# Dense products of an attention and FFN layer: one plain fp32 matmul per product in place of three matmuls of rounded high and low parts

## The reference

```
xn = layernorm(x)                                   # no gain, no bias
s  = attention(xn)                                  # 16 heads of 16, RoPE, causal softmax, q k v and output products 256x256
h  = fwht(xn * SU_ug) / 64                          # Walsh-Hadamard transform over 256
h  = silu(h @ W_gate.T * a) * (h @ W_up.T * b)      # 256 -> 1024
h  = fwht(h * SU_dp) / 64                           # over 1024
g  = silu(h @ W_down.T * c)                         # 1024 -> 256
out = x + s * g
```

## Time and profile before

| what | value |
|---|---|
| time, median of 3 runs | 804.27 us (802.99 to 805.4) |
| span of the profiled execution, first to last instruction | 804.6 us |
| busy in the span: PE, DVE, ACT, POOL | 787.2, 566.7, 497.8, 411.1 us |
| weight loads on PE | 482.7 us |
| mean granted TensorE clock | 0.993 |

### The profile page before, as it was taken

The page is one execution under the profiler, slowest core; times in us unless marked ns, Lnnn a source line. Parts: engine busy times, 40 slices in busy tenths (PEclk is TensorE's granted clock), DMA queues, the critical chain, the costliest instruction groups (busy, mean ns, idle before and its releaser), DMA issues. The chain is left out here.

```text
span 804.6 us, 14554 instructions
## 1 busy us (share of the span) xinstructions
PE 787.2 (98%) x5232; PEld 482.7 (60%) x5232; DVE 566.7 (70%) x1021; ACT 497.8 (62%) x686; POOL 411.1 (51%) x472
## 2 busy tenths in 40 slices
PE   8999999999999999999999999999999999999987
PEld 4678788888766555555555555555555555555545
DVE  5875545456686777777777777777777777777736
ACT  4576355463544777667777665677766677666472
POOL 3878678574742463321765434267453236746233
PEclk9999999999999999999999999999999999999997
DMA  9262444354541222333333453334344333445121
GB/s 319 84 199 96 158 156 158 106 131 145 182 113 39 65 77 60 91 107 107 103 107 110 122 171 93 95 108 132 115 114 142 98 105 95 133 130 170 67 87 70
DMA packets 61248, 95.71 MB, mean 119 GB/s; under 512 B 10553, under 2 KB 27641, under 8 KB 61177
## 3 DMA queue, kind: packets, MB, share of 16 engines
q1 hardware_dynamic: 59176, 92.42, 38.0%
q10 hardware_dynamic: 2000, 2.36, 0.9%
HBM read 57.54 MB, written 36.95 MB: 117 GB/s over the span
## 5 line engine op out<-in xcount | busy, mean ns | idle before, releaser
L1564 ACT ACTIVATE probs<-ps 128x1024 f32<-128x1024 f32 (+1 forms) x320 | 292.0, 938 | 93.7 <-PE ps L1391 92.0
L1686 DVE TENSOR_REDUCE mx<-ps 128x4 f32<-128x1024 f32 (+1 forms) x192 | 216.1, 1134 | 58.9 <-PE ps L1368 37.2
L1249 POOL TENSOR_SCALAR_AFFINE_SELECT probs<-probs 128x256 f32<-128x256 f32 (+1 forms) x192 | 92.6, 485 | 255.1 <-ACT probs L1564 254.5
L1681 DVE CUSTOM_DVE_ANT_0 ps<-ps,tri 128x512 f32<-128x512 f32 (+1 forms) x256 | 153.8, 652 | 48.4 <-PE ps L1368 48.3
L1413 PE MATMUL ps<-probs,v_ones 128*32 128x512 f32 (+3 forms) x1584 | 157.0, 486 | 0.1
L1391 PE MATMUL ps<-q_s,k_s 64*128 64x512 f32 (+3 forms) x768 | 143.7, 399 | 3.8 <-ACT probs L1564 1.4
L1368 PE MATMUL ps<-k_s,q_s 48*128 48x512 f32 (+3 forms) x768 | 134.7, 381 | 4.1 <-DVE mx L1686 0.8
L1391 PEld LDWEIGHTS ps<-q_s,k_s 64*128 64x128 f32 x768 | 67.0, 184 | 103.9 <-issue 53.6
L1368 PEld LDWEIGHTS ps<-k_s,q_s 48*128 48x128 f32 x768 | 69.5, 185 | 63.6 <-ACT probs L1564 38.2
L343 PE MATMUL ps<-xh,wug_hi 128*128 128x512 f32 x256 | 105.6, 413 | 1.0 <-DVE rot L898 1.0
L398 POOL TENSOR_TENSOR a_sb<-a_sb,u_sb 128x512 f32<-128x512 f32 x64 | 82.4, 1295 | 41.7 <-ACT u_sb L371 20.9
(11 more groups left out here) (151 smaller groups left out, 1061.5 us busy)
## 6 DMA issues: line engine op xcount, KB each, us to landing
scr_qk<-kinds SPq DMA_DIRECT2D x64, 256.0 KB, 2.4
q_s<-scr_qk SPq DMA_DIRECT2D x64, 128.0 KB, 2.8
k_s<-scr_qk SPq DMA_DIRECT2D x64, 128.0 KB, 3.0
scr_heads<-o_raw SPq DMA_DIRECT2D x30, 256.0 KB, 2.1
scr_v<-v_st SPq DMA_DIRECT2D x16, 256.0 KB, 2.9
q_s<-scr_qk SPq DMA_DIRECT2D x64, 64.0 KB, 3.0
k_s<-scr_qk SPq DMA_DIRECT2D x64, 64.0 KB, 3.1
v_raw<-scr_v SPq DMA_DIRECT2D x16, 256.0 KB, 2.8
```

Source lines behind the costliest of these rows:

```text
L1249: pool.affine_select(out=part, in_=part, compare_op=ALU.is_ge, fill=0.0, base=0, pattern=pattern, channel_multiplier=-1).then_inc(cut, 1)
L1564: act.activation(probs[:, n % 2, p, :, 0:w], ps[:, bank:bank + 2, 0:w], ACT.Exp, scale=SCALE).then_inc(exp_ok, 1)
L1681: last = dve.tensor_tensor_reduce(part_of, part_of, sh.tri[:, CH - w:CH], 1.0, LOWEST, ALU.add, ALU.max, mx[:, v % 2, kind, h, i % TPC:i % ...
L1686: last = dve.tensor_reduce(out[:, :, pairs[0]:pairs[0] + n], ps[:, banks[0]:banks[0] + 2, 0:n * w].rearrange('p e (x k) -> p e x k', x=n), ...
```

## The change

Every operand is kept once, in plain fp32: `wug`, `wd`, `wqkv`, `wo`, `wo_end`, `xt`, `hid`. Each product is one plain fp32 matmul. All roundings and subtractions that made the parts go, with their semaphores. `hidden` now writes to `hid` and takes over the wait for the downs of the FFN chunk before. `take_xh` becomes `take_x`, a copy in plain fp32 by ACT. The weights that were scratch views over other tiles (`late`, `res`) become tiles of their own or views of `wug`; the reload of x goes to `x_res`, after a wait for the results of the chunk before. The rounds, the jobs in them and the PSUM banks stay.

```diff
-        self.hid_hi = nc.alloc_sbuf_tensor_at('hid_hi', [P, IB, CH], F32R, offset=HID_AT)
-        self.hid_lo = nc.alloc_sbuf_tensor_at('hid_lo', [P, IB, CH], F32R, offset=HID_AT + 4 * IB * CH)
+        self.hid = sb('hid', [P, IB, CH])
...
-        self.wug_hi = sb('wug_hi', [P, DC, 2 * INTER], F32R)
-        self.wug_lo = sb('wug_lo', [P, DC, 2 * INTER], F32R)
-
-        self.late = nc.alloc_sbuf_tensor_at('late', [P, 5 * DC, CH], F32, offset=WUG_AT)
-        self.wd_hi = sb('wd_hi', [P, IB, D], F32R)
-        self.wd_lo = sb('wd_lo', [P, IB, D], F32R)
-        self.xh = sb('xh1', [P, DC, CH], F32R)
-        self.xl = sb('xl1', [P, DC, CH], F32R)
+        self.wug = sb('wug', [P, DC, 2 * INTER])
+        self.wd = sb('wd', [P, IB, D])
+        self.xt = sb('xt1', [P, DC, CH])
...
 def ffn_features(pe, ps, sh, bank, ib, first_col, done):
     cols = slice(first_col + ib * P, first_col + (ib + 1) * P)
-    terms = [(w, a, d) for d in range(DC)
-             for w, a in ((sh.wug_hi, sh.xh), (sh.wug_hi, sh.xl), (sh.wug_lo, sh.xh))]
-    for m, (w, a, d) in enumerate(terms):
-        last = pe.matmul(ps[:, bank, :], w[:, d, cols], a[:, d, :], start=m == 0, stop=m == len(terms) - 1)
+    for d in range(DC):
+        last = pe.matmul(ps[:, bank, :], sh.wug[:, d, cols], sh.xt[:, d, :], start=d == 0, stop=d == DC - 1)
     last.then_inc(done, 1)
 
 
 def ffn_down(pe, ps, sh, bank, n, o, q):
     per = IB // QUARTERS
-    pe.wait_ge(sh.hl_ok, nth_hid(n, per * (q + 1)))
+    pe.wait_ge(sh.hid_ok, nth_hid(n, per * (q + 1)))
     cols = slice(o * P, (o + 1) * P)
     for ib in range(per * q, per * (q + 1)):
-        for k, (w, h) in enumerate(((sh.wd_hi, sh.hid_hi), (sh.wd_hi, sh.hid_lo), (sh.wd_lo, sh.hid_hi))):
-            last = pe.matmul(ps[:, bank, :], w[:, ib, cols], h[:, ib, :], start=ib == 0 and k == 0,
-                             stop=ib == IB - 1 and k == 2)
+        last = pe.matmul(ps[:, bank, :], sh.wd[:, ib, cols], sh.hid[:, ib, :], start=ib == 0, stop=ib == IB - 1)
     last.then_inc(sh.down_ok, 1)
...
     if m >= NA:
-        act.wait_ge(sh.hl_ok, m - NA + 1)
+        act.wait_ge(sh.hid_ok, m - NA + 1)
...
-    pool.tensor_tensor(sh.a_sb[:, m % NA, :], sh.a_sb[:, m % NA, :], sh.u_sb[:, m % NUP, :],
+    if n:
+        pool.wait_ge(sh.down_ok, nth_down(n - 1, DC - 1, ib // (IB // QUARTERS)) + 1)
+    pool.tensor_tensor(sh.hid[:, ib, :], sh.a_sb[:, m % NA, :], sh.u_sb[:, m % NUP, :],
                        op=ALU.mult).then_inc(sh.hid_ok, 1)
-
-
-def wait_hidden(eng, sh, n, ib):
-    eng.wait_ge(sh.hid_ok, nth_hid(n, ib) + 1)
-    if n:
-        eng.wait_ge(sh.down_ok, nth_down(n - 1, DC - 1, ib // 2) + 1)
-
-
-def hidden_low(pool, sh, n, ib):
-    m = nth_hid(n, ib)
-    pool.wait_ge(sh.hh_ok, m + 1)
-    pool.tensor_tensor(sh.hid_lo[:, ib, :], sh.a_sb[:, m % NA, :], sh.hid_hi[:, ib, :].bitcast(F32),
-                       op=ALU.subtract).then_inc(sh.hl_ok, 1)
...
-                    terms = [(w, a, d) for d in range(DC)
-                             for w, a in ((wqkv_hi, xh[par]), (wqkv_hi, xl[par]), (wqkv_lo, xh[par]))]
-                    for m, (w, a, d) in enumerate(terms):
-                        last = pe.matmul(ps[:, bank + o, :], w[:, d, cols], a[:, d, :], start=m == 0,
-                                         stop=m == len(terms) - 1)
+                    for d in range(DC):
+                        last = pe.matmul(ps[:, bank + o, :], wqkv[:, d, cols], xt[par][:, d, :], start=d == 0,
+                                         stop=d == DC - 1)
...
-                        terms = [(a, w, d) for d in range(DC)
-                                 for a, w in ((xh[par], wqkv_hi), (xh[par], wqkv_lo), (xl[par], wqkv_hi))]
-                        for m, (a, w, d) in enumerate(terms):
-                            last = pe.matmul(ps[:, bank + n, t * D:(t + 1) * D], a[:, d, tok], w[:, d, 2 * D:],
-                                             start=m == 0, stop=m == len(terms) - 1)
+                        for d in range(DC):
+                            last = pe.matmul(ps[:, bank + n, t * D:(t + 1) * D], xt[par][:, d, tok], wqkv[:, d, 2 * D:],
+                                             start=d == 0, stop=d == DC - 1)
...
-            def weights_high(i):
+            def scale_weights(i):
                 bank = pair_at['W', i]
                 act.wait_ge(prod, i + 1)
                 act.wait_ge(scale_ok, 2)
                 if i < NUG:
                     for o in range(DC):
                         cols = slice(UG_PARTS[i] * PART, (UG_PARTS[i] + 1) * PART)
-                        last = act.mul(sh.wug_hi[:, o, cols], ps[:, bank + o, :], su_ug_s[:, o:o + 1])
+                        last = act.mul(sh.wug[:, o, cols], ps[:, bank + o, :], su_ug_s[:, o:o + 1])
...
-            def take_xl(c):
-                bank = pair_at['X', c]
-                dve.wait_ge(xh_ok, c + 1)
-                dve.tensor_tensor(xl[c % 2][:, :, :], ps[:, bank:bank + 2, :], xh[c % 2][:, :, :].bitcast(F32),
-                                  op=ALU.subtract).then_inc(xl_ok, 1)
...
-        wo_hi = sb('wo_hi', [P, DC, D], F32R)
-        wo_lo = sb('wo_lo', [P, DC, D], F32R)
+        wo = sb('wo', [P, DC, D])
+        wo_end = sb('wo_end', [P, D])
...
-        o_hi = sb('o_hi', [P, DC, CH], F32R)
-        o_lo = sb('o_lo', [P, DC, CH], F32R)
-
+        o_end = sb('o_end', [P, DC, CH])
+        x_res = sb('x_res', [P, DC, CH])
...
                 eng.wait_ge(scaled, ch + 1)
-                eng.wait_ge(low, ch + 1)
+                if ch:
+                    eng.wait_ge(res_ok, DC * ch)
                 for o in range(DC):
                     eng.wait_ge(sh.y_out[o], 16 * (NTH_FFN[ch] + 1))
                 eng.dma_start(spread_of(ch), scr['gate'][ch].rearrange('o p n -> p o n')).then_inc(more_in[ch % 2], 16)
-                eng.dma_start(heads_of(ch), xt_d[ch]).then_inc(more_in[ch % 2], 16)
+                eng.dma_start(x_res[:, :, :], xt_d[ch]).then_inc(more_in[ch % 2], 16)
...
-                pe.wait_ge(high, ch + 1)
-                pe.wait_ge(low, ch + 1)
+                if ch == LAST:
+                    pe.wait_ge(last_scaled, 1)
+                else:
+                    pe.wait_ge(scaled, ch + 1)
                 if ch == 0:
-                    pe.wait_ge(wo_ok, 1)
+                    pe.wait_ge(wo_in, 16)
                 cols = slice(o * P, (o + 1) * P)
                 whole = groups_of(ch) == NG
-                terms = [(w, a, d) for d in range(DC)
-                         for w, a in ((wo_hi, high_of(ch)), (wo_lo, high_of(ch)), (wo_hi, low_of(ch)))]
-                for n, (w, a, d) in enumerate(terms):
+                for d in range(DC):
                     rows = slice(0, rows_of(ch, d))
-                    last = pe.matmul(ps[:, bank_of[turn], queries], w[rows, d, cols], a[rows, d, queries], start=n == 0,
-                                     stop=whole and n == len(terms) - 1)
+                    last = pe.matmul(ps[:, bank_of[turn], queries], wo[rows, d, cols], heads_of(ch)[rows, d, queries],
+                                     start=d == 0, stop=whole and d == DC - 1)
                 if whole:
                     last.then_inc(piece_ok, 1)
 
             def end_piece(m, o):
-                pe.wait_ge(fin_high, m + 1)
-                if m == 1:
-                    pe.wait_ge(early_low, 1)
-                else:
-                    pe.wait_ge(fin_low, 1 + m // 2)
+                pe.wait_ge(divided, m + 1)
+                pe.wait_ge(end_in, 16 * HG)
                 ch, queries = FIN[m]
                 c = ch % QC
                 cols = slice(o * P, (o + 1) * P)
-                terms = ((end_hi, fin_hi), (end_lo, fin_hi), (end_hi, fin_lo))
-                for n, (w, a) in enumerate(terms):
-                    last = pe.matmul(ps[:, end_bank(m, o), queries], w[:, cols], a[:, c, queries], start=False,
-                                     stop=n == len(terms) - 1)
-                last.then_inc(piece_ok, 1)
+                pe.matmul(ps[:, end_bank(m, o), queries], wo_end[:, cols], o_raw[c][:, queries], start=False,
+                          stop=True).then_inc(piece_ok, 1)
...
-            def high_part(ch):
-                act.wait_ge(scaled, ch + 1)
-                act.copy(high_of(ch), heads_of(ch)).then_inc(high, 1)
-
-            def end_high(m):
-                ch, queries = FIN[m]
-                act.wait_ge(divided, m + 1)
-                act.copy(fin_hi[:, ch % QC, queries], o_raw[ch % QC][:, queries]).then_inc(fin_high, 1)
...
                     take_heads()
-                    high_part(LAST - 1)
                     invert(LAST)
-                    low_part(LAST - 1)
...
                 if z == END + 3:
-                    end_high(0)
-                    end_low(0)
                     scale_heads(LAST)
-                    high_part(LAST)
-                    low_part(LAST)
             for o in range(DC):
                 gate_piece(LAST - 1, o)
```

(74 more changed lines are left out.)

145 lines of the change are left out of this document (32 added, 113 removed).

## The result

| | before | after |
|---|---|---|
| time, median of 4 runs each | 804.12 us | 880.46 us (879.16 to 881.39) |
| ratio, 95% interval | | 1.0945 (1.0929 to 1.0962) |
| span of the profiled execution | 804.6 us | 877.4 us |

The change costs 76.3 us by the medians, 72.8 by the two profiled spans. In every recorded execution of both kernels the time lies 1.7 to 1.8 us above the span (879.16 beside 877.4). So the profiled execution of before took about 806.4 us in the count of the timed runs: 2.2 above the median and not 0.3, and one of its slowest. Its mean clock was 0.993. Executions of before with a clock of 0.999 or 1.000 have spans of 800.7 to 801.6; the two of the changed kernel with 0.999 have 877.4 and 877.9, 76 to 77 us more. Readings between the two traces come out up to 3.5 us low. Where sizes matter I go by the timed ratios.

What follows compares the result with a forecast made beforehand. TensorE was taken as the bound: 804.6 + 89.5 for dearer products - 3 for waits - 3 at the end = 888.1 us profiled, so 887.8 for the timed median; range 876 to 899 for 8 in 10.

Steps and rivals of the forecast that it cites:

- The bound: TensorE, busy 98%, bounds from some 10 us after the start to the last 15 us; its work moves the end one for one.
- That the splitting counts for nothing: Casts, subtractions and roundings removed from POOL, ACT and DVE lie under PE's work, so removing them itself saves nothing.
- The price of a plain product: One plain fp32 product, read from the weight folds: 0.857 us for 512 columns in two records, 0.43 estimated for 256.
- second rival: A plain product of 512 columns costs half, 0.43 us, giving 673 us; chance 0.02 together with the third rival.
- The price of three matmuls: Three fp32r matmuls per product before: 0.684 us for 512 columns, 0.341 for 256; surcharges of plain form 0.173 and 0.09.
- Waits given back: Of PE's 11 us of waits for ACT, DVE and POOL, longer rounds return 3 us, bounds 0 and 9.
- The window 700 to 780: Window with 2.7 us without PE, read as without row-maximum tiles, where ACT's exponentials are close behind.
- Changes of form: Entering dense matmuls from half-array ones, some 150 runs at 0.11 us: no extra for plain fp32, upper bound 16 us.
- fourth rival: Plain fp32 costs more than in the folds, by a second exposed load on entry or falling clock: 904 us; chance 0.11.
- The end: After the last heads: inversion starts 1 us earlier, about 2 us less after the last division; 3 us saved, bounds 1 and 5.

Runs made afterwards that it cites:

- run 1: Kernel before with all splitting kept, each product one plain fp32 matmul of the high parts, low terms left out: 882.49 us, ratio 1.0967.
- run 2: Changed kernel without splitting, three fp32r matmuls per FFN, q, k and v product, output pieces plain fp32: 805.09 us, ratio 1.0008 against the kernel before.
- run 5: Four kernels: the one before, splitting kept, plain fp32 in one kind of product: gate and up 844.35, downs 823.17, q, k, v 817.34, output pieces 809.15 us.
- run 3: As run 2, but four fp32r matmuls per FFN, q, k and v product, no splitting: 909.19 us, ratio 1.1318 against the kernel before.
- run with plain output pieces: Kernel before, splitting kept, plain fp32 matmuls of the high parts in the output pieces and last heads only: 809.15 us, ratio 1.0068.
- run with the downs alone: Kernel before, splitting kept, plain fp32 matmuls of the high parts in the FFN downs only: 823.17 us, ratio 1.0230.
- run with features alone: Kernel before, splitting kept, plain fp32 matmuls of the high parts in the FFN gate and up products only: 844.35 us, ratio 1.0517.
- q, k and v alone: Kernel before, splitting kept, plain fp32 matmuls of the high parts in the q, k and v products only: 817.34 us, ratio 1.0147.
- run 4: As run 2, but one fp32r matmul per FFN, q, k and v product, then two: 724.04 us (ratio 0.8996) and 731.75 us (0.9112).

## Why the prediction came out as it did

**The bound**: right. PE at 98% became 99%, and its longer products make the time. That the splitting counts for nothing was nearly right: it is worth 1.8 us with the plain form, not clear of nothing, and 4.8 with three matmuls (runs 1, 2 and 5).

**The price of a plain product**: right to 0.002 us, and the two records were one product. The second rival (a product costs half) fell. The Trainium skill, Perfetto Trace Analysis, section Engine Utilization, halves the array's output rate of 307.2 G elements per second for fp32 in low and high parts; 128 x 512 elements take 0.213 us at its full rate and 0.427 at half, an estimate from the page. Each of the two records ran at that half rate; the whole product, 0.859 us, took four times the 0.213. The Trainium skill's section Identifying the Most-Contended Engine on the same page judges TensorE's headroom by the share of weight loads, beside the arithmetic done; that share fell here from 60 to 45%, which by itself reads as more headroom, and the time rose 9.5%.

**The price of three matmuls**: mis-sized. I took it from short stretches: 0.228 us per matmul, and 0.1135 for v. Whole runs are slower. From before's timeline, the first chunk's q and k products and a later chunk's v products:

```profile
16.05 0.52 PE L667 MATMUL ps<-xh,wqkv_hi 128*128 128x512 f32 x1
...
21.64 1.02 PE L708 MATMUL ps<-raw,had 128*128 128x512 f32 x2
...
74.38 0.36 PE L681 MATMUL ps<-wqkv_hi,xh 128*128 128x256 f32 x1
...
77.32 0.40 PE L667 MATMUL ps<-xh,wqkv_hi 128*128 128x512 f32 x1
```

24 matmuls in 5.59 us are 0.233 each, 0.699 for three, and the product's surcharge 0.159 and not 0.173. 24 of the v form in 2.94 are 0.123, 0.368 for three, and the surcharge 0.064 and not 0.09. On 64 products each that is 0.9 and 1.7 us. A part of v's is not price. Where an fp32r matmul follows a plain one, this trace starts it early, and the plain product's second record is cut short by as much:

```profile
28.53 1.02 PE L709 MATMUL ps<-raw,minus_had 128*128 128x512 f32 x2
28.99 0.68 PE L681 MATMUL ps<-wqkv_hi,xh 128*128 128x256 f32 x1
29.51 0.27 PE L681 MATMUL ps<-wqkv_lo,xh 128*128 128x256 f32 x1
```

The fold takes 0.46 us here in place of 0.86, the first v matmul 0.52 in place of 0.12. Before has two such places, and three behind the transposes with 0.08 each; 1.0 us of its 23.7 us of v belongs to the row everything else, and v's surcharge is 4.9 us.

For gate and up the mean over all 256, entries and exits included, rose by 0.170 (184.5 to 227.9), 0.9 us in sum. Over all products the surcharge start to start was 79.4 us and not 89.5. The other 6.6 us of this are in the downs and in the output pieces, 3.3 each, and most of them are the clock in the one profiled execution of before, as shown below. With its products taken from traces where the clock did not fall on them (downs 93.0, output pieces 29.4, v 22.7) the surcharge is 85 us, an estimate. So over all products the surcharge was 4.5 us less than forecast. That and the waits make the error.

**Waits given back**: right in kind, too small. I took 3 us with 0 to 9 as bounds, from the waits view. Scores and maxima gave back 7.7, of which mask matmuls took 1.4 again: 3.3 more than forecast. The reason I gave, longer rounds, is the one that run 3 shows; relief of ACT, DVE and POOL, the theory I tested first, is not it: with all splitting kept, run 1 has 105.7 and 99.3 us in scores and maxima, the changed kernel 106.0 and 99.4. The window 700 to 780 was misread: it holds row-maximum tiles up to 761.8.

**Changes of form**: zero, nearly as taken. An entry costs 0.10 us with the plain form and 0.11 with fp32r, under 1 us over all. The number of runs was misread: the 80 long distances in line 343 are not all entries. About 50 are entries (0.34 us) and 30 exits (0.32). Over all dense products 87 runs stand behind half-array matmuls, not some 150. Nothing in the sum hung on it, only the bound of the fourth rival, which did not come.

**The end**: the size came near by luck (2.1 us against 3), the mechanism was wrong. The last product with the values starts 13.9 us before the end of the span before. After it is 11.8 us. I put that down to the casts and subtractions that go. The run with plain output pieces and run 1 keep them and end just as early. The timelines of PE, in the order before, after, run 1, output pieces alone, with spans 804.6, 877.4, 880.8 and 807.3:

```profile
790.69 0.86 PE L1413 MATMUL ps<-probs,v_ones 128*32 128x256 f32 x16
```

```profile
865.62 0.86 PE L1294 MATMUL ps<-probs,v_ones 128*32 128x256 f32 x16
```

```profile
869.00 0.86 PE L1407 MATMUL ps<-probs,v_ones 128*32 128x256 f32 x16
```

```profile
795.48 0.86 PE L1413 MATMUL ps<-probs,v_ones 128*32 128x256 f32 x16
```

It is 11.8 us in each of the three with plain products. What differs with them is the clock. Windows of before and of the run with output pieces alone (clock third from the end):

```profile
795.00:800.00 5.00, 4.10 (x18) 3.48 (x19) 3.32 (x6) 0.81 (x2) 2.13 (x3) 0.65 0.18 66
800.00:805.00 5.00, 1.03 (x5) 0.74 (x4) 1.64 (x4) 0.00 (x0) 0.00 (x0) 0.50 0.32 105
```

```profile
795.00:800.00 5.00, 5.00 (x32) 2.59 (x31) 4.96 (x6) 0.78 (x2) 3.13 (x3) 1.00 0.25 91
800.00:805.00 5.00, 3.72 (x14) 2.16 (x14) 3.74 (x9) 0.40 (x1) 1.50 (x3) 1.00 0.20 69
```

Before, the clock falls from 2.4 to 1.2 GHz in this stretch; with plain output products TensorE is busy without a gap up to 800, and the clock stays at 2.4. But the plain form is not needed for that. The run with the downs alone has the three-matmul end of before, with the same gaps, and its clock stays up in the same stretch:

```profile
809.40:814.40 5.00, 4.07 (x26) 3.23 (x25) 4.46 (x7) 0.81 (x2) 2.02 (x4) 1.00 0.28 105
```

There the last product with the values starts 12.4 us before the end, in the runs with features and with q, k and v alone, also at the upper clock, 12.1 and 12.2. From that product to the last gate on DVE it is 10.4 us before, 8.2 to 8.5 in these three and 8.3 in the changed kernel. So 1.5 to 1.8 of the 2.1 us go with the clock of the profiled execution of before, and 0.3 to 0.6 are left for the change. Why the clock fell in one execution and not in the others is open.

Two readings behind my 3 us were wrong as well. Before, 14 matmuls start between the last division and the last gate, not 18. After, there are six products behind the last division (it ends at 870.62), not two, since TensorE takes its work in order:

```profile
870.60 1.13 PE L1346 MATMUL ps<-o_raw,wo_end 128*128 128x256 f32 x4
871.57 1.22 PE L1335 MATMUL ps<-wug,wo 128*128 128x256 f32 x4
872.72 1.13 PE L1346 MATMUL ps<-o_raw,wo_end 128*128 128x256 f32 x4
```

Without the casts the last division ends 5.0 us after the last product with the values, and 6.1 to 6.4 in the three runs named. The last gate then follows after 3.3 us, in those three after 2.1: the longer products take back what the casts gave.

**A dip of the clock** that I had in view and did not use: the 0.98 of 205 to 300. From 240 to 244 the clock of before is mostly at its lower level, after a stretch in which PE had waited for row maxima:

```profile
236.00:240.00 4.00, 2.69 (x23) 1.71 (x20) 3.47 (x8) 1.57 (x3) 0.00 (x0) 1.00 0.19 68
240.00:244.00 4.00, 4.00 (x11) 3.17 (x12) 2.72 (x6) 0.00 (x0) 0.00 (x0) 0.57 0.43 131
```

TensorE was in the downs, so 0.43 x 4 = 1.7 us of the downs' 95.7 is this dip. The trace of the changed kernel has no such dip, that of run 1 has one and that of run 2 two, those of the runs with features or downs alone have none. Each is one execution; the others of before have mean clocks from 0.993 to 1.000. The dip explains 1.7 of the downs' missing 3.3 us in the traces, and half of the 3.4 us between the spans of run 1 and the changed kernel. In the run with features alone the downs of before, without a dip, took 93.0 us and not 95.7. The output pieces of before took 29.4 or 29.5 us in the three traces whose clock stayed up at the end, and 31.3 in the trace of before.

**Traces against timed runs.** The 3.5 us between the spans' difference and the medians' are the choice of execution: the profiled one of before is 2.2 us above its median, the one of the changed kernel 1.3 below. The plain output pieces took 3.0 us more of the profile and 5.5 of the timed runs; against the 29.4 us at the upper clock it is 4.9.

**Open**: q, k and v alone cost 11.8 us where the traces differ by 15.2 in them (10.3 and 4.9); 1.8 of the difference is the end, 12.2 us in that run's trace and 13.9 in that of before, the rest is not explained. The estimate of 85 us less what the rounds gave back, 6.3, is 78.7, 2 us above the 76.3 measured. And only 1.4 us of the 4.8 that the splitting costs with three matmuls have a place in the traces.

## What to carry to other kernels

Price both forms over whole runs of matmuls, start to start, from the longest stretch of the trace; on an engine that is busy in 98% the difference times the count is close to the answer (85 us here, of which longer rounds gave 6 back; measured 76), and taking the splitting from the other engines was worth 0.2 to 0.6%. Look at the clock of both traces before taking a small difference between them as an effect of the change. On this engine a plain fp32 product costs as much as 3.7 fp32r matmuls of 512 columns: three of them (805 us) beat it (880), four (909) do not. If the result bears the rounding of one fp32r pass, one matmul per FFN, q, k and v product without splitting (run 4) is faster than both kernels, 724 us, but two already reach 732. By its waits DVE's row maxima come next; making them cheaper was not tried.

## What the runs showed of the hardware that was not expected

A plain fp32 product of 256 columns cost 0.432 us, half of one of 512, while three fp32r ones cost 0.34 to 0.36 by the run: the fp32r form varies a little (0.113 to 0.120 per matmul of 256 columns, the early starts behind plain products set right), the plain form does not (3.45 or 3.46 us in all eight chunks). Its records follow one another at 0.215 us, more than the 0.19 us of a weight load, those of the fp32r form at 0.12; whether that is the cause was not tried. Executions of one and the same kernel differed in mean clock (0.993 to 1.000 before) and in span, on one chip by 3 us, and at the end three matmuls at 2.4 GHz reached the last gate as soon as one plain matmul did.
